# Values' products of layer 0 for two blocks of keys together, every fourth slot, with six probability buffers in place of four

## The reference

```python
# layer 0: group norm (32 groups), 8 heads of 32 channels
h = groupnorm(x) * gn_w + gn_b
q, k, v = split(qkv_w @ h + qkv_b)          # per head: 32 x 1024 each
w = softmax((q * s).T @ (k * s))            # s = 32 ** -0.25; 1024 x 1024 per head
a = v @ w.T                                 # values' products
x1 = x + proj_w @ a + proj_b
# layer 1: one head, keys and queries of 32 channels, values of 256
q, k, v = Wq @ x1, Wk @ x1, Wv @ x1
out = gamma * (v @ softmax(q.T @ k).T) + x1
```

## Time and profile before

| | |
|---|---|
| median of 3 runs | 1871.88 us |
| span of the profiled execution | 1863.5 us |
| median over that span | 8.4 us |
| PE busy | 1624.4 us, 87% |
| DVE busy | 1496.4 us, 80% |
| POOL busy | 1146.0 us, 61% |
| ACT busy | 822.1 us, 44% |
| mean granted clock of PE | 0.916 |

### The profile page before, as it was taken

The page is one execution under the profiler, slowest core; times in us unless marked ns, Lnnn a source line. Parts: engine busy times, 40 slices in busy tenths (PEclk is TensorE's granted clock), DMA queues, the critical chain, the costliest instruction groups (busy, mean ns, idle before and its releaser), DMA issues.

```text
span 1863.5 us, 25934 instructions
## 1 busy us (share of the span) xinstructions
PE 1624.4 (87%) x7120; PEld 910.2 (49%) x7120; DVE 1496.4 (80%) x2108; ACT 822.1 (44%) x1501; POOL 1146.0 (61%) x528
## 2 busy tenths in 40 slices
PE   4988999997999879998899978999789997989867
PEld 2534444572445634465345644457344573445426
DVE  2898798888888878879888797887978888785644
ACT  2255445533454344543455334553445534444402
POOL 2278686746677456765676665775576745786803
PEclk9689899998999989999899998999889998998979
DMA  4313030301303031020403004030130302200100
GB/s 123 71 44 69 2 91 18 69 12 47 88 11 69 17 88 51 20 50 18 121 18 69 2 17 121 18 69 7 40 93 18 69 12 56 65 1 1 46 17 23
DMA packets 38746, 85.78 MB, mean 46 GB/s; under 512 B 10304, under 2 KB 20416, under 8 KB 38592
## 3 DMA queue, kind: packets, MB, share of 16 engines
q1 hardware_dynamic: 38208, 82.88, 17.7%
q0 software_dynamic: 384, 1.05, 0.2%
HBM read 18.29 MB, written 8.39 MB: 14 GB/s over the span
## 4 chain that ended last, share of the span: by engine, by line
PE 57%; DVE 25%; issue 14%; ACT 1%; DVEq 1%; DMA 1%; SPq 1%; POOL 0%; ACTq 0%
PE st L463 11%; PE pv L472 10%; DVE mpart L812 10%; PE work L517 10%; PE pv L494 8%; PE work L585 5%; DVE raw L919 3%; DVE rec L904 3%; PE work L549 3%; DVE rec L915 2%; PE work L592 2%; PE work L561 2%; PE work L555 2%; PE work L538 2%; DVE mpart_l L815 2%
## 5 line engine op out<-in xcount | busy, mean ns | idle before, releaser
L788 POOL TENSOR_TENSOR acc<-acc,probs 128x1024 f32<-128x1024 f32 x352 | 837.1, 2402 | 223.3 <-ACT probs L651 223.1
L651 ACT ACTIVATE probs<-st 128x512 f32<-128x512 f32 x1152 | 619.5, 598 | 609.2 <-PE st L463 492.6
L812 DVE TENSOR_REDUCE mpart<-work 128x1 f32<-128x512 f32 x1024 | 644.7, 681 | 143.3 <-PE work L517 140.8
L517 PE MATMUL work<-ks,qs 96*128 96x512 f32 x1024 | 426.5, 491 | 103.0 <-DVE mpart L812 73.1
L463 PE MATMUL st<-qs,ks 98*128 98x512 f32 x1024 | 392.7, 465 | 25.3 <-ACT probs L651 12.7
L463 PEld LDWEIGHTS st<-qs,ks 98*128 98x128 f32 x1024 | 190.0, 205 | 304.8 <-ACT probs L651 143.8
L517 PEld LDWEIGHTS work<-ks,qs 96*128 96x128 f32 x1024 | 203.9, 205 | 225.0 <-DVE mpart L812 127.5
L788 POOL TENSOR_TENSOR acc<-probs 128x1024 f32<-128x1024 f32 x64 | 152.1, 2387 | 257.7 <-ACT probs L651 257.6
L472 PE MATMUL pv<-probs,vt 128*32 128x512 f32 x2048 | 304.4, 669 | 0.1
L494 PE MATMUL pv<-probs,l_vt 128*128 128x256 f32 x1024 | 253.6, 383 | 5.6 <-ACT raw L724 5.2
L494 PEld LDWEIGHTS pv<-probs,l_vt 128*128 128x128 f32 x1024 | 190.1, 190 | 44.5 <-issue 9.9
(11 more groups left out here) (77 smaller groups left out, 1197.0 us busy)
## 6 DMA issues: line engine op xcount, KB each, us to landing
qs<-part_hi SPq DMA_DIRECT2D x124, 128.0 KB, 2.4
ks<-part_hi SPq DMA_DIRECT2D x124, 128.0 KB, 2.4
xa<-in_x SPq DMA_DIRECT2D x16, 512.0 KB, 4.2
qs<-part_lo SPq DMA_DIRECT2D x64, 128.0 KB, 2.4
ks<-part_lo SPq DMA_DIRECT2D x64, 128.0 KB, 2.4
y<-in_x SPq DMA_DIRECT2D x8, 1024.0 KB, 5.4
out<-raw SPq DMA_DIRECT2D x32, 256.0 KB, 2.2
qs<-mrow SPq DMA_DIRECT2D x256, 2.0 KB
```

The lines of the kernel that those rows point to most:

```text
L517: last = mm(bank, qs[g][0:HI_HI_LO, j, t0:t0 + P], ks[g][0:HI_HI_LO, j, half * HALF:(half + 1) * HALF], start=True, stop=True)
L651: nc.scalar.activation(probs[:, n % PRING, half * HALF:(half + 1) * HALF], st[:, (2 * n + half) % ST_BANKS, :], ACT.Exp).then_inc(s_exp1 i ...
L788: pool.tensor_tensor(a, first, probs[:, n % PRING, :], ALU.add).then_inc(s_add0, 1)
L812: last = dve.reduce_max(mpart[:, 4 * j + tb, half:half + 1], bank, AX.X)
```

## The change

Bursts of layer 0 are issued two at a time, in every fourth slot (n % 4 == 1), for the units of slots n - 4 and n - 2. The bursts of slots 3, 7, 11, ... move to the slots 5, 9, 13, ... two slots later; those of slots 5, 9, ... stay. Since a buffer of `probs` is now read up to two slots later, the ring has six buffers. The first burst of a chunk, with its wait for the bank `pv`, moves from its third to its fifth slot along with the first product.

```diff
-PRING = 4
+PRING = 6
...
                     if n == 1 and kind not in ("prologue", "first"):
+                        product_l0(SLOTS - 3, b - 1)
                         product_l0(SLOTS - 1, b - 1)
-                    elif n % 2 and n - 3 in units and unit_use(n - 2)[0] == 0:
+                    elif n % 4 == 1 and n - 3 in units and unit_use(n - 2)[0] == 0:
                         ci = unit_use(n - 2)[1] // 16
-                        if unit_use(n - 2)[1] % 16 == 1:
+                        if unit_use(n - 2)[1] % 16 == 3:
                             pv_free(ci, kind, b)
...
+                        product_l0(n - 4, b)
                         product_l0(n - 2, b)
```

## The result

The kernel after takes 1885.35 us (median of four runs, 1883.30 to 1889.17), the kernel before 1872.3 (1869.36 to 1873.25): ratio 1.0081, interval 1.0058 to 1.0104. It is slower by 13 us as the medians stand and by 15 (11 to 19) as the ratio has it, where the prediction had 6. The profiled execution has a span of 1883.3 us and a time of its own of 1885.13.

A forecast was written before the change was run, and what follows sets the result against it. Prediction: PE and DVE take turns over four banks, neither full, so only places where one waits count. Gains 5.7, losses 6.5 per batch, 7 batches, about 6 us: 1869.5 plus 8.4, 1878 us; range 1875 to 1890.

The forecast's parts named there:

- The price of a burst: On PE, a burst alone costs 1.18 us, the second of two together 0.86, so two together save 0.32.
- the ceiling of 41 us: Most PE time the change could save: 127 mergers at 0.32 us each, 2.2% of the span.
- The step that failed: Slots 5, 17, 21, 37, 53 to 58 and 65: DVE's own work bridges the burst, nothing gained or lost.
- What would show it: Signs in the profile after: bursts of sixteen at 1.85 us, DVE's and PE's waits, the chain, the branch, the mean clock.
- the ledger: Slot-by-slot sum over a steady batch: 0.8 to 0.9 us later per batch, 7 batches, about 6 us slower.
- the rival "nothing to see": Whole kernel: gains and losses within 0.2% (3.7 us), 1868 to 1875.6 us; chance 0.20.
- The gains: Where DVE waits behind a dropped burst: slots 67 (1.4), 7 (2.0), 23 (1.8), small waits 0.5; 5.7 us per batch.
- the losses: Slots 61, 1, 69, 9, 25, 29, 13, 41 and 45, where double bursts leave DVE dry: 6.5 us per batch.
- The loop's edge: Last burst of a batch was free inside PE's 2.60 us branch time; moved to slot 1 it costs 0.86 us.
- The half-clock rival: Dropped bursts at slots 7, 23, 67 total 5.2 us per batch; with half the losses, 1855 us; chance 0.28.
- The clock rival: PE's clock falls more often: two more half-clock spells per batch cost 26 us, giving 1904 us; chance 0.10.
- The 8.4 us: Median of the runs shown, 1871.88, over the profiled span; carried over from 1869.5 to reach 1878 us.

The follow-up runs named there:

- Without the collision: The kernel after, with POOL's first addition of the second chunk (slot 18) waiting until DVE's normalization chain is done: 1873.35 us, ratio 1.0008.
- the control with the same wait: The kernel before, with POOL's slot 18 addition waiting for DVE's normalization chain: 1869.91 us, ratio 0.998.
- three merges: The kernel before with six buffers, POOL waiting for the normalization, and double bursts only at slots 9, 25 and 69: 1872.81 us, ratio 0.9992.
- the second attempt: The kernel before, with eight tiny DVE copies between aff_a and mua of the normalization in steady batches: 1901.24 us, ratio 1.0139.
- six pairs: Double bursts only at slots 9, 13, 17, 25, 41 and 69, six buffers, POOL waiting for the normalization, against the kernel before: 1852.23 us, ratio 0.9914.

## Why the prediction was right on the side and short in size

- **The price of a burst** held in the main: a second one costs 0.86 to 0.87, as forecast. A burst that goes brings the slots behind it 1.08 us forward where nothing waits (1.18 forecast), so two together save 0.22 and not 0.32, and the ceiling of 41 us was 28.
- **The step that failed** is "The other slots (5, 17, 21, ...) have DVE work of their own to bridge the burst: nothing either way." Behind slot 17 the change loses 2.76 us at once and 2.3 per round in the end, 13.7 us in all by the ratios. The part went through PE's order and DVE's waits for PE. That "what ACT, POOL and DVE run keeps its order" is true of each engine by itself, but when POOL's addition starts is set by PE, through ACT's exponentials; that the two meet in time was not looked at. "What would show it" has no line for it either.
- **The sum of the rest** is not decided. Without the collision the kernel is 1.5 us over before (interval -1.7 to 4.7), where the ledger has 6, and 5 over the control with the same wait (about -1 to 11). Its median, 1873.35, is in the range of the rival "nothing to see" and below the forecast's 1875 to 1890. That the time of the change, 1885.35, fell into that range was luck: the small loss forecast came out as slower by a meeting that is in no term of the sum.
- **The gains were mostly right where they stand, the losses too small, and neither adds up.** Without the collision slot 8 gained 2.4 within slot 7 (forecast 2.0), slot 68 gained 1.25 within slot 67 (1.4), and slot 2 was 0.83 late (0.86). Slot 45 cost 2.6, beyond its bounds of 0.86 to 1.7, and slot 61 cost 1.7, at the end of them; the first runs wholly or mostly at half clock, sixteen instructions in 2.9 to 3.65 us in every round, with and without the collision, where the single burst before took 1.40 and, by the timeline of all rounds, 1.06 to 1.59. Slots 25 and 26 lose 2.1 in place of 0.5, since what slot 24 gains is spent in the next wait for DVE. Slots 5, 21 and 37 lose 0.4, 0.8 and 0.6 more than slots 3, 19 and 35 gain, where "nothing" stood. The loop's edge, 0.86, is real in slot 2 and gone by slot 10. With three merges the gains forecast at 21 us gave none; six gave 16 to 20 of the 31 that their sites had shown.
- **The half-clock rival** asked for three dear bursts to decide; of their 5.2 us per batch, with three merges, slot 8 gained its 2.0, slot 24 gave back what it gained and slot 68 gained 0.4. **The clock rival** was in part true: the double bursts of slots 45 and 61 run wholly or mostly at half clock in every round (2.9 to 3.65 us), and slots 18 to 24 have more of it with the collision; the mean granted clock is 0.909, between that rival's mark of 0.89 and the 0.916 of before, and 0.914 without the collision.
- **The signs named**: the double burst at 1.85 came, and the chain lost PE and gained DVE. Of the waits behind slots 1, 9, 13, 29 and 41, those of slots 2 and 10 doubled or more, slot 14 went from 0.38 to 0.57, slot 30 from 0.21 to 0.95, slot 42 stayed (0.59 and 0.57). PE's waits for L814 rose by 7.5 us in the matmuls' row (80.6, before 73.1) and by 22 in the loads' (149.9, before 127.5), rows that can hold the same wait twice, where 4 per batch were forecast. The waits at 714.73 and 759.84 did not go, they are 1.17 and 1.21. The pv group did change, by 22 us. The branch did not move forward: the edge takes 4.67 to 4.95 us before and 4.74 to 5.07 after. These signs could not tell the cause: DVE's wait for L517 is 162.1 without the collision, 159.6 with it and 140.8 before.
- **The 8.4 us** that the prediction adds to the span are no time around it: after, the run's own time is 1.83 over its span, and in the runs of the experiments it is 1.8 too. So the profiled execution of before was a short one; the two spans differ by 19.8 us, the medians by 13. The forecast is not touched by it, since 1871.88 + 6 is 1878 as well.

The Trainium skill, "GPSIMD Engine Reference", section "Specifications", states that GpSimd shares its SBUF interfaces with VectorE and contends with instructions that have two SBUF inputs or run in a 2-port mode. The rows of mua, 2.24 to 2.26 us in place of 0.16 with two inputs, agree. The copies of the second attempt have one input and were held too; in which mode they ran no row here says. The price is read from the rows: not a share, but the whole rest of POOL's instruction.

## What to carry to other kernels

Read each place where a short operation of one engine stands within a few tenths of a microsecond of a long one of another that it shares a path with; a change that moves either decides who goes first, and here it was decided the same way in all six rounds of the loop. In a kernel where two engines take turns, a term read at one slot is worth nothing until it has been followed to the next wait: place all slots of both kernels against one start and look where the difference steps. Undo a schedule change site by site before giving it up, since the 32 bursts of a batch merged everywhere cost 13 us (15 by the ratio) and six pairs, with one wait on POOL, gain 20 (16 by the ratio).

## What the runs showed of the hardware

- A DVE operation with two inputs in SBUF that starts while POOL adds ends behind POOL's instruction, however short it is: mua by 0.02 us, 2.24 to 2.26 in place of 0.16; L909, of 128 columns, by 0.15. In the trace after, the 102 products of L909 that start inside an addition take 1.38 us on average, the 26 others 0.29; the reciprocals of L906, with one input, take 0.94 inside and outside. A tiny copy from SBUF to SBUF stood still as well. The other way round POOL starts beside a running DVE operation and does not hold it up (aff_b before, 0.16).
- The granted clock of slots 44 to 48 differs between rounds of one program. In the kernel before the stretch from slot 44 to slot 48 takes 9.05 us at 1.00, 10.25 at 0.83 and 11.6 to 11.8 at 0.71 to 0.73; with merges at 9, 25 and 69 rounds of 1.00 and of 0.62 to 0.73 differ by about 3 us in length. Six rounds of that are about the size of the spread that the kernel before shows over its runs (1860 to 1885 us); that the one is the cause of the other was not tried.

The kernel before pays the price of the first point too, at another place. Its page:

```profile
L904 DVE RECIPROCAL rec<-rec 128x128 f32<-128x128 f32 x128 | 120.5, 941 | 41.4 <-ACT rec L678 41.3
L907 DVE TENSOR_TENSOR attn<-attn,rec 128x128 f32<-128x128 f32 x128 | 149.4, 1167 | 4.4
```

Of the 128 products of L907, 100 start inside an addition and take 1.41 us on average, the 28 others 0.29: 112 us of DVE's busy time. So the price stood in the page of before, as a mean of 1167 ns. Whether those 112 us lie where the end is set was not tried.
